# Local attention layers: where the turn of the probabilities, its copy and the copy of the values stand in the slot

## Chip, cores and metric

The kernel runs on one core of one Trainium2 chip. The metric is the device time of one execution in microseconds. Names used: TensorE (PE; its weight loads are PEld), VectorE (DVE), ScalarE (ACT), GpSimd (POOL), SyncE (SP, which only issues DMAs here).

## What is computed

A batch of 16 sequences of 128 tokens with 128 features goes through several residual blocks. The change lies in the second one, six layers of local attention with 16 heads of 64, each followed by a feed-forward block (FFN):

```python
for i in range(DEPTH):                                   # DEPTH = 6
    x = attn_layer(shift_tokens(x), Wqkv[i], q_scale[i], k_scale[i], Wo[i]) + x
    x = ffn_layer(shift_tokens(x), ln_g[i], ln_b[i], W1[i], b1[i], W2[i], b2[i]) + x

def attn_layer(x, Wqkv, qs, ksc, Wo):
    q, k, v = split_heads(x @ Wqkv)
    q = l2norm(q) * qs ; k = l2norm(k) * ksc
    q, k = rotary(q, scale), rotary(k, 1 / scale)
    sim = (q @ k.T) * 8                  # each window of 32 sees itself and the one before
    out = softmax(mask(sim)) @ v
    return out @ Wo
```

Ahead of it stand a conditioned causal attention and a rotation of images, behind it a gated linear attention and two mixtures of experts.

## The kernel before

The local layers are cut into `LOCAL` = 384 ticks t: 6 layers, 16 sequences, 4 groups of 4 heads. They run as a software pipeline over slots u. In slot u every engine runs its function `slot(u)`, in which each stage handles the tick t = u - L of that stage (`L_QKV` = 1 to `L_PROJ` = 9, line 75). The order within a slot is written out by hand on each engine, and each engine's queue runs strictly in that order; semaphores tie the engines together.

- TensorE (`pe_local`): `queries` (L1181, into `qk_ps`), `turn_probs` (L1170, transposes of the probabilities `pr` into `pTl_ps`), deferred projections, `turn_queries` (L1188, into `turn_ps`), one step of an FFN chunk, `values` (L1244, into `vl_ps`), `score` (L1209 the mask, L1215 the products), `attend` (L1233), `project` (L1198).
- ScalarE (`act_local`): the copy of the values (`vt`, L1536, for the tick whose values TensorE made one slot earlier, `L_MOVE` = 6), four exponentials (L1545), the copy of the turned probabilities (`pT`, L1554), the copy of the attention output (`oT`, L1561), the squares of queries and keys (L1568), in every fourth slot the shift of the next sequence (`xs`, L1507 and L1509), steps of the FFN (its shift `xf`, squares, Gelus), the copy of the turned queries and keys (`qkT`, L1586).
- VectorE (`dve_local`): FFN steps, the sum `qr` of the two rope products (L1398), the cosine product (L1409), `rec` (L1417), the normalization `qn` (L1425), the sums of squares (L1433, L1437), the maximum (L1445). Around a Gelu (`bursts`) it makes the copies of `pT`, `oT`, `qkT` and `vt` in ScalarE's place.
- GpSimd (`pool_local`): scaling of the probabilities by `rec` (L1597), the sine product (L1607), the power for the norms (L1617), the power of the FFN's variance (L1624).
- SyncE: after each values copy it spreads parts of `vt` into `vx` with four DMAs (L565), after the attention of the tick two before.

`vl_ps` and `pTl_ps` lie in one PSUM bank, `bank[4]` (L279). So `turn_probs` of a slot waits until the values of the slot before are copied (`v_moved`), and `values` waits until the turned probabilities of its slot are copied (`pT_moved`). `sl_ps` and `ol_ps`, the scores and the attention output, share banks too, so `maximum` waits for `attend`. The values rotate through three of four allocated buffers (`vt[t % 3]`), and the copy into one waits for the attention of tick t - 3 (`o_ready`) and for its spread.

An FFN chunk (four sequences) starts every 16 slots from u = 25. Its steps: shift 0, mean 1, squares 2, variance 3, spread 6, gate 7 to 9, Gelu 10, up 11 to 13, down 14 to 16.

Of the kernel before, what the change touches and what calls it, by code (L numbers as in the profile page):

```python
# [22 lines left out]
GROUPS = 4  # L23
# [51 lines left out]
L_QKV, L_ROPE, L_COS, L_SUM, L_TURN, L_SCORE, L_V, L_MOVE, L_EXP, L_PROB, L_PROJ = 1, 2, 3, 4, 5, 6, 5, 6, 7, 8, 9  # L75
# [181 lines left out]
def build(nc, d, out):  # L257
    with ExitStack() as ctx:
# [184 lines left out]
        def live(t):  # L443
            return 0 <= t < LOCAL

        @block.sync
        def _(sp):
# [109 lines left out]
            for t in range(LOCAL + 32):  # L557
                if live(t):
                    near, far = vt[t % 3], vx[t % 2]
# [604 lines left out]
        def pe_local(pe):  # L1164
# [56 lines left out]
            def attend(t, u):  # L1221
# [5 lines left out]
                for k, (_, lo, hi) in enumerate(SPANS):  # L1227
                    for r in range(2):
                        for pair in range(2):
                            row = slice(pair * HD, (pair + 1) * HD)  # L1230
                            at = SLOT_V[k][pair] * P + r * HD
                            values = vt[t % 3] if k == 2 * pair else vx[t % 2]
# [63 lines left out]
            def slot(u):  # L1296
                if live(u - L_QKV):
                    queries(u - L_QKV)
                if live(u - L_PROB):
                    turn_probs(u - L_PROB, u)  # L1300
# [24 lines left out]
        def dve_local(dve):  # L1325
# [129 lines left out]
            def slot(u):  # L1455
# [35 lines left out]
                if live(t) and bursts(u):  # L1491
                    dve.wait_ge(a.v_ready, TICKS + t + 1)
                    dve.wait_ge(a.o_ready, TICKS + t - 2)
                    dve.wait_ge(a.v_spread[(t - 3) % 2], 64 * ((t - 3) // 2 + 1))
                    dve.tensor_copy(vt[t % 3][:, :], vl_ps).then_inc(a.v_moved, 1)
# [8 lines left out]
        def act_local(act):  # L1504
# [23 lines left out]

            def slot(u):
                t = u - L_MOVE  # L1530
                if live(t) and not bursts(u - 1):
                    act.wait_ge(a.v_ready, TICKS + t + 1)
                    act.wait_ge(a.o_ready, TICKS + t - 2)
                    if t >= 3:
                        act.wait_ge(a.v_spread[(t - 3) % 2], 64 * ((t - 3) // 2 + 1))
                    act.copy(vt[t % 3][:, :], vl_ps).then_inc(a.v_moved, 1)  # L1536
                t = u - L_EXP
                if live(t):
# [5 lines left out]
                    for h in range(GH):  # L1544
                        ex = act.activation(pr[t % 2][:, h * BAND:(h + 1) * BAND],  # L1545
# [4 lines left out]
                t = u - L_PROB  # L1550
                if live(t) and not bursts(u) and not bursts(u - 1):
                    act.wait_ge(a.pT_ready, TICKS + t + 1)
                    act.wait_ge(a.o_ready, TICKS + t - 1)
                    act.copy(pT[t % 2][:, 0:GB], pTl_ps).then_inc(a.pT_moved, 1)  # L1554
# [28 lines left out]
                if live(t) and not bursts(u):  # L1583
                    act.wait_ge(a.qkT_ready, t + 1)
                    act.wait_ge(a.sc_ready, TICKS + t - 1)
                    act.copy(qkT[t % 2][:, :], turn_ps[:, :]).then_inc(a.qkT_moved, 1)  # L1586
            for u in range(TAIL):
                slot(u)
# [850 lines left out]
```

## Time and profile before

| | us |
|---|---|
| median of 3 runs | 2542.26 |
| lowest, highest | 2539.84, 2543.18 |
| profiled execution, its own time | 2539.52 |
| span of its trace | 2537.7 |
| granted TensorE clock, mean | 0.989 |

| stretch, us | what runs |
|---|---|
| 0 to 507 | causal attention, images |
| 507 to 560 | the pipeline of the local layers fills |
| 560 to 2180 | local layers, one slot in 3.4 to 5.6 us |
| 2180 to 2537 | linear attention and experts |

The page's lines in the section on rows are read so: an engine's busy time and its share of the span; the chain is followed back from the last instruction, at each step to what released it. "issue" in it is time for which the profile shows no releaser. In timelines a matmul's length includes its latency, so starts, not lengths, show how densely they follow each other; the chain shows the time that each adds.

### The profile page before, as it was taken

Reading aid. Unit: us, or ns where it says so; the run is one execution under the profiler, and the core shown is the slowest. Engines: PE = TensorE matmul, PEld = TensorE weight load, DVE = VectorE, ACT = ScalarE, POOL = GpSimd, SP = SyncE. Lnnn points to the kernel's source line nnn. Section 1 sums busy time; section 2 is a strip of 40 time slices with the busy share of each in tenths; the row PEclk is TensorE's granted clock in tenths of the full one; section 3 lists DMA queues with packets and bytes.
Section 4 is the critical chain, followed back from the end, with each engine's and each line's share of the span. In section 5 each row is a group of like instructions: output and inputs, shape, how many; then the busy total and the mean of one; then the engine's idle time right before and its main releaser. Section 6 shows DMA issues by size and latency. Waiting matters only on the chain.

```text
span 2537.7 us, 98074 instructions
## 1 busy us (share of the span) xinstructions
PE 2406.5 (95%) x36438; PEld 1705.4 (67%) x36442; DVE 1999.7 (79%) x4388; ACT 1885.7 (74%) x6630; POOL 1764.7 (70%) x1605
## 2 busy tenths in 40 slices
PE   7999888879999999999999999999999999799999
PEld 6888555546666666666666666666666766377874
DVE  5555699978888888888888888888888888555644
ACT  4777899868888888888888888888888888533323
POOL 2888887488888888888888878888888888122200
PEclk9999999999999999999999999999999999899999
DMA  4100210021112111211112111211121111100000
GB/s 123 15 15 15 51 14 13 10 85 37 32 34 66 38 36 33 58 42 43 33 41 59 41 33 33 66 39 36 34 58 43 42 33 34 30 1 1 1 1 17
DMA packets 177876, 91.06 MB, mean 36 GB/s; under 512 B 40974, under 2 KB 174328, under 8 KB 177408
## 3 DMA queue, kind: packets, MB, share of 16 engines
q1 hardware_dynamic: 168574, 80.42, 11.8%
q0 software_dynamic: 8192, 4.21, 1.4%
q8 instruction: 298, 4.88, 0.8%
q14 instruction: 170, 1.39, 0.2%
q10 hardware_dynamic: 642, 0.15, 0.0%
HBM read 30.57 MB, written 3.76 MB: 14 GB/s over the span
## 4 chain that ended last, share of the span: by engine, by line
PE 82%; DVE 10%; issue 5%; POOL 2%; ACT 1%; SPq 0%; DMA 0%; DVEq 0%; POOLq 0%; ACTq 0%
PE bank L1181 13%; PE bank L1198 9%; PE scores L1233 7%; PE bank L1244 7%; PE bank L1188 6%; PE scores L1215 6%; PE bank L1170 3%; PE bank L1273 3%; PE bank L1291 2%; PE bank L1282 2%; PE bank L639 2%; PE scores L1209 2%; DVE rg_prod L1011 2%; PE scores L671 2%; PE bank L1915 1%
## 5 line engine op out<-in xcount | busy, mean ns | idle before, releaser
L1617 POOL TENSOR_TENSOR rs<-ssc,neg_half 128x8 f32<-128x8 f32 x384 | 644.0, 1677 | 39.0 <-DVE ssc L1437 39.0
L1607 POOL TENSOR_TENSOR t_pair<-qn_pair,tabs 128x512 f32<-128x512 f32 x384 | 489.1, 1274 | 12.2 <-DVE qn_pair L1425 11.6
L1545 ACT ACTIVATE pr<-scores,negmax 128x64 f32<-128x64 f32 x1536 | 461.6, 313 | 48.2 <-DVE negmax L1445 23.5
L1597 POOL TENSOR_TENSOR pr<-pr,rec 128x256 f32<-128x256 f32 x384 | 235.5, 613 | 282.3 <-DVE rec L1417 282.3
L1181 PE MATMUL bank<-wqk,xs 128*128 128x512 f32 x768 | 402.5, 606 | 12.5 <-DVE qn_pair L1425 11.2
L1545 ACT ACTIVATION_READ_ACCUMULATOR pr<-scores,negmax 128x1 f32 x1536 | 311.5, 203 | 0.0
L1080 POOL DMA_INDIRECT rg_win<-rg_images,share_down x256 | 255.3, 997 | 76.7 <-issue 56.4
L1433 DVE TENSOR_REDUCE ss<-sq 128x8 f32<-128x512 f32 x384 | 260.9, 679 | 34.0 <-ACT sq L1568 32.8
L1425 DVE TENSOR_TENSOR qn_pair<-bank,rs 128x512 f32<-128x512 f32 x384 | 257.1, 669 | 27.0 <-POOL rs L1617 26.8
L1536 ACT COPY vt<-bank 128x256 f32<-128x256 f32 x361 | 135.2, 374 | 186.8 <-issue 186.5
L1198 PE MATMUL bank<-oT,wo 128*128 128x128 f32 x1536 | 266.1, 296 | 0.0
L1398 DVE TENSOR_TENSOR qr_pair<-t_pair 128x512 f32<-128x512 f32 x384 | 265.6, 692 | 0.3 <-issue 0.2
L1409 DVE TENSOR_TENSOR t_pair<-qn_pair,tabc 128x512 f32<-128x512 f32 x384 | 262.9, 685 | 0.0
L1568 ACT ACTIVATE sq<-bank 128x512 f32<-128x512 f32 x384 | 241.8, 630 | 13.9 <-PE bank L1181 13.9
L1445 DVE TENSOR_REDUCE negmax<-scores 128x4 f32<-128x256 f32 x384 | 162.9, 424 | 108.8 <-PE scores L1233 100.1
L1244 PE MATMUL bank<-wv,xs 128*128 128x256 f32 x768 | 236.6, 390 | 10.2 <-ACT pT L1554 3.2
L1170 PEld LDWEIGHTS bank<-ident,pr 128*128 128x128 f32 x768 | 107.5, 141 | 201.1 <-issue 197.8
L1188 PE MATMUL bank<-ident,qr_pair 128*128 128x128 f32 x1536 | 230.9, 273 | 0.0
L1244 PEld LDWEIGHTS bank<-wv,xs 128*128 128x128 f32 x768 | 131.8, 190 | 135.7 <-issue 132.0
L1586 ACT COPY qkT<-bank 128x512 f32<-128x512 f32 x361 | 219.4, 608 | 3.1 <-PE bank L1188 0.3
L1233 PE MATMUL scores<-pT,vt 64*64 64x64 f32 (+1 forms) x3072 | 211.8, 231 | 0.6 <-ACT oT L1561 0.4
L1198 PEld LDWEIGHTS bank<-oT,wo 128*128 128x128 f32 x1536 | 200.5, 190 | 13.3 <-issue 0.5
(313 smaller groups left out, 5503.7 us busy)
## 6 DMA issues: line engine op xcount, KB each, us to landing
rg_prod<-vt SPq DMA_DIRECT2D x1536, 32.0 KB, 1.9
wqk<-in_L_ffn_Wqkv SPq DMA_DIRECT2D x20, 256.0 KB
rg_win<-rg_images,share_down POOLq DMA_INDIRECT x256
wv<-in_L_ffn_Wqkv SPq DMA_DIRECT2D x20, 128.0 KB
wo<-in_L_ffn_Wo SPq DMA_DIRECT2D x20, 128.0 KB, 2.5
w<-in_L_ffn_W SPq DMA_DIRECT2D x6, 341.0 KB
rg_images<-rg_prod SPq DMA_DIRECT2D x1, 1625.0 KB, 7.7
ZT<-in_x SPq DMA_DIRECT2D x4, 256.0 KB, 4.0
```

Source lines behind the costliest of these rows:

```text
L1181: pe.matmul(qk_ps[t % 2][:, :], xs[b % 2][:, :], wqk[:, g, :, :].rearrange("p i n -> p (i n)"), start=True, stop=True).then_inc(a.qk_ready, 1)
L1188: mm = pe.transpose(turn_ps[:, c * P:(c + 1) * P], qr[t % 2][:, c * P:(c + 1) * P], ident[:, :])
L1198: mm = pe.matmul(yl_ps, wo[:, 2 * g + c, :], oT[b % 2][:, (2 * g + c) * P:(2 * g + c + 1) * P], start=(g == 0 and c == 0), stop=(g == GROU ...
L1233: mm = pe.matmul(ol_ps[r * HD:(r + 1) * HD, pair, lo:hi], values[row, at:at + HD], pT[t % 2][row, r * P + lo:r * P + hi], start=True, stop ...
L1244: pe.matmul(vl_ps, xs[b % 2][:, :], wv[:, g * GV:(g + 1) * GV], start=True, stop=True)\
L1398: dve.tensor_tensor(qr[t % 2][:, :], t1[t % 2][:, :], t2[t % 2][:, :], ALU.add)\
L1409: dve.tensor_tensor(t1[t % 2][:, :].rearrange("p (i h e) -> p i h e", i=2, h=GH), qn[t % 2][:, :].rearrange("p (i h e) -> p i h e", i=2, h ...
L1425: dve.tensor_tensor(heads(qn[t % 2][:, :]), heads(qk_ps[t % 2][:, :]), over(rs[t % 2][:, :], [P, 8, HD], 2), ALU.mult).then_inc(a.normed, 1)
L1433: dve.tensor_reduce(ss[t % 2][:, :, 0], heads(sq[t % 2][:, :]), AX.X, ALU.add).then_inc(a.summed, 1)
L1545: ex = act.activation(pr[t % 2][:, h * BAND:(h + 1) * BAND], sl_ps[:, h // 2, h % 2 * BAND:(h % 2 + 1) * BAND], ACT.Exp, bias=negmax[t % 2 ...
L1607: pool.tensor_tensor(t2[t % 2][:, :].rearrange("p (i h f e) -> p i h f e", i=2, h=GH, f=2), qn[t % 2][:, :].rearrange("p (i h f e) -> p i ...
L1617: pool.tensor_tensor(rs[t % 2][:, :], ssc[t % 2][:, :], neg_half[:, 0:8], ALU.pow)\
```

## The change

TensorE runs `turn_probs` ahead of `queries` in its slot. ScalarE copies the turned probabilities between its second and third exponential instead of after the fourth (where a slot has exponentials). The copy of the values moves from the head of ScalarE's next slot to the end of the slot in which TensorE makes them, behind the copy of `qkT`. The values rotate through four buffers, so their copy waits for the attention and the spread of tick t - 4. Slots next to a Gelu keep their copies on VectorE, where only the buffer and the waits of the values copy change.

```diff
-                    near, far = vt[t % 3], vx[t % 2]
+                    near, far = vt[t % GROUPS], vx[t % 2]
...
             def slot(u):
+                if live(u - L_PROB):
+                    turn_probs(u - L_PROB, u)
                 if live(u - L_QKV):
                     queries(u - L_QKV)
-                if live(u - L_PROB):
-                    turn_probs(u - L_PROB, u)
...
                     dve.wait_ge(a.v_ready, TICKS + t + 1)
-                    dve.wait_ge(a.o_ready, TICKS + t - 2)
-                    dve.wait_ge(a.v_spread[(t - 3) % 2], 64 * ((t - 3) // 2 + 1))
-                    dve.tensor_copy(vt[t % 3][:, :], vl_ps).then_inc(a.v_moved, 1)
+                    dve.wait_ge(a.o_ready, TICKS + t - 3)
+                    dve.wait_ge(a.v_spread[t % 2], 64 * (t // 2 - 1))
+                    dve.tensor_copy(vt[t % GROUPS][:, :], vl_ps).then_inc(a.v_moved, 1)
...
+            def pT_copy(u):
+                t = u - L_PROB
+                if live(t) and not bursts(u) and not bursts(u - 1):
+                    act.wait_ge(a.pT_ready, TICKS + t + 1)
+                    act.wait_ge(a.o_ready, TICKS + t - 1)
+                    act.copy(pT[t % 2][:, 0:GB], pTl_ps).then_inc(a.pT_moved, 1)
+
             def slot(u):
-                t = u - L_MOVE
-                if live(t) and not bursts(u - 1):
-                    act.wait_ge(a.v_ready, TICKS + t + 1)
-                    act.wait_ge(a.o_ready, TICKS + t - 2)
-                    if t >= 3:
-                        act.wait_ge(a.v_spread[(t - 3) % 2], 64 * ((t - 3) // 2 + 1))
-                    act.copy(vt[t % 3][:, :], vl_ps).then_inc(a.v_moved, 1)
                 t = u - L_EXP
...
                     for h in range(GH):
+                        if h == GH // 2:
+                            pT_copy(u)
                         ex = act.activation(pr[t % 2][:, h * BAND:(h + 1) * BAND],
...
                     ex.then_inc(a.exp_ready, 1)
-                t = u - L_PROB
-                if live(t) and not bursts(u) and not bursts(u - 1):
-                    act.wait_ge(a.pT_ready, TICKS + t + 1)
-                    act.wait_ge(a.o_ready, TICKS + t - 1)
-                    act.copy(pT[t % 2][:, 0:GB], pTl_ps).then_inc(a.pT_moved, 1)
+                else:
+                    pT_copy(u)
...
                     act.copy(qkT[t % 2][:, :], turn_ps[:, :]).then_inc(a.qkT_moved, 1)
+                t = u - L_V
+                if live(t) and not bursts(u):
+                    act.wait_ge(a.v_ready, TICKS + t + 1)
+                    act.wait_ge(a.o_ready, TICKS + t - 3)
+                    if t >= 4:
+                        act.wait_ge(a.v_spread[t % 2], 64 * (t // 2 - 1))
+                    act.copy(vt[t % GROUPS][:, :], vl_ps).then_inc(a.v_moved, 1)
```

## Rows read from the trace of the kernel before

**Rows 1.** The page: busy time by engine, then the chain that ended last, by engine.
```profile
PE 2406.5 (95%) x36438; PEld 1705.4 (67%) x36442; DVE 1999.7 (79%) x4388; ACT 1885.7 (74%) x6630; POOL 1764.7 (70%) x1605
...
PE 82%; DVE 10%; issue 5%; POOL 2%; ACT 1%; SPq 0%; DMA 0%; DVEq 0%; POOLq 0%; ACTq 0%
```

**Rows 2.** Busy time by stretch: window, length, then PE, PEld, DVE, ACT, POOL, clock.
```profile
560.00:2050.00 1490.00, 1462.52 (x25577) 1025.19 (x25576) 1290.02 (x2871) 1237.99 (x4753) 1223.57 (x1060) 1.00 0.16 42
```

**Rows 3.** Timeline of ScalarE in a short slot: start us, us, line, out<-in.
```profile
1040.63 0.39 ACT L1554 COPY pT<-bank 128x256 f32<-128x256 f32 x1
1040.88 0.42 ACT L1561 COPY oT<-scores 128x256 f32<-128x256 f32 x1
```

**Rows 4.** The chain that ended last: start us, length us, what ran on it.
```profile
1040.95 0.16 issue
1041.12 0.67 PE bank L1244 x2
...
1054.29 0.43 PE bank L1244 x2
...
1067.14 0.95 issue
...
2142.44 0.67 PE bank L1244 x2
```

**Rows 5.** Timelines of TensorE and ScalarE around slots 15, 0 and 1.
```profile
1087.18 0.38 ACT L1536 COPY vt<-bank 128x256 f32<-128x256 f32 x1
1091.53 0.38 ACT L1536 COPY vt<-bank 128x256 f32<-128x256 f32 x1
...
1087.42 1.02 PE L1181 MATMUL bank<-wqk,xs 128*128 128x512 f32 x2
1088.28 0.38 PE L1170 MATMUL bank<-ident,pr 128*128 128x128 f32 x2
...
1091.30 1.12 PE L1181 MATMUL bank<-wqk,xs 128*128 128x512 f32 x2
```

**Rows 6.** The same behind slot 3.
```profile
1035.09 0.38 ACT L1536 COPY vt<-bank 128x256 f32<-128x256 f32 x1
1035.33 1.02 PE L1181 MATMUL bank<-wqk,xs 128*128 128x512 f32 x2
```

**Rows 7.** Timeline of the one slot in which the turn came late.
```profile
606.65 0.38 ACT L1536 COPY vt<-bank 128x256 f32<-128x256 f32 x1
607.17 0.41 PE L1170 MATMUL bank<-ident,pr 128*128 128x128 f32 x2
607.42 0.60 PE L1188 MATMUL bank<-ident,qr_pair 128*128 128x128 f32 x4
```

**Rows 8.** Timelines of VectorE, GpSimd and TensorE in slots 4 to 7.
```profile
1036.94 0.17 DVE L1417 RECIPROCAL rec<-sums 128x4 f32<-128x4 f32 x1
1039.27 0.68 DVE L1398 TENSOR_TENSOR qr_pair<-t_pair 128x512 f32<-128x512 f32 x1
1043.23 0.73 DVE L1398 TENSOR_TENSOR qr_pair<-t_pair 128x512 f32<-128x512 f32 x1
1045.50 0.69 DVE L1425 TENSOR_TENSOR qn_pair<-bank,rs 128x512 f32<-128x512 f32 x1 [0.64 <-POOL rs L1617]
1048.08 0.55 DVE L1358 TENSOR_SCALAR rg_prod<-rg_prod,cols 128x512 f32<-128x512 f32 x1
...
1037.19 0.61 POOL L1597 TENSOR_TENSOR pr<-pr,rec 128x256 f32<-128x256 f32 x1 [1.14 <-DVE rec L1417]
1039.00 1.64 POOL L1617 TENSOR_TENSOR rs<-ssc,neg_half 128x8 f32<-128x8 f32 x1
1040.60 1.01 POOL L1624 TENSOR_TENSOR xr<-xv,neg_half 128x4 f32<-128x4 f32 x1
1043.37 2.09 POOL L1617 TENSOR_TENSOR rs<-ssc,neg_half 128x8 f32<-128x8 f32 x1
...
1048.77 1.09 PE L1273 MATMUL bank<-rg_prod,w 128*128 128x512 f32 x2
```

More of the change, by code:

```diff
@@ L72 @@
 TABLES_AT = (4, 6, 7, 8)
-L_QKV, L_ROPE, L_COS, L_SUM, L_TURN, L_SCORE, L_V, L_MOVE, L_EXP, L_PROB, L_PROJ = 1, 2, 3, 4, 5, 6, 5, 6, 7, 8, 9
+L_QKV, L_ROPE, L_COS, L_SUM, L_TURN, L_SCORE, L_V, L_EXP, L_PROB, L_PROJ = 1, 2, 3, 4, 5, 6, 5, 7, 8, 9
 FFN_FIRST, FFN_EVERY = TICKS // NCH + L_PROJ, TICKS // NCH
@@ L1231, in attend @@
                             at = SLOT_V[k][pair] * P + r * HD
-                            values = vt[t % 3] if k == 2 * pair else vx[t % 2]
+                            values = vt[t % GROUPS] if k == 2 * pair else vx[t % 2]
                             mm = pe.matmul(ol_ps[r * HD:(r + 1) * HD, pair, lo:hi], values[row, at:at + HD],
```

## Prediction

> **What bounds the kernel now.** I read the page's busy times and its chain first: TensorE is busy 95% of the span and carries 82% of the chain that ended last [rows 1]. The busy table by stretch places it: the local layers run from about 507 to 2180 us, and between 560 and 2050 us TensorE is busy 1462.5 of 1490 us at full clock, while ScalarE, VectorE and GpSimd have 1238, 1290 and 1224 us of work [rows 2]. So the change can win only what TensorE's chain loses to waits, and it can cost whatever new wait it puts into TensorE's queue. Then I read the chain piece by piece and the four timelines slot against slot. The FFN chunks repeat every 16 slots; I number the slots 0 to 15 from the one where a chunk starts (u = 25, 41, ...). There are 23 such periods.
>
> In a slot with no FFN work ahead of the values (slots 4 and 5, and most of those before u = 25), `values` waits for the copy of the turned probabilities, because both live in one bank. The copy starts behind all four exponentials at 1040.63 and ends at 1041.02 [rows 3]; the chain shows 0.16 us of nothing, then 0.67 us for the two values matmuls, where an unhindered pair takes 0.43 [rows 4]. The difference is a weight load that nothing covers. There are 58 pieces of 0.67 in the chain from 557 us to the last at 2142 [rows 4]. The other wait, 0.95 us in slot 11 [rows 4], is for exponentials that stand behind the Gelus and their table loads. The change doesn't touch it.
>
> **Part 1: the copy of the turned probabilities between the exponentials.** It then starts after two exponentials, some 0.6 us earlier, and the queue position that it takes is 0.25 us (1040.63 to 1040.88) [rows 3]. That removes both pieces of the stall: 0.13 to 0.16 us plus 0.24, say 0.37 us in each of 58 slots, 21 us. This is all that the change can win. Two such slots stand in every period (0.74 us), 14 before the first FFN chunk. The price: the last two exponentials end 0.25 us later, and with them `rec`, on which GpSimd waits.
>
> **Part 2: the turn at the head of TensorE's slot.** No work is added. But the turn waits for the values copy of the slot before (the shared bank), and in front of that wait stood the queries: the turn began 0.86 us after them (1087.42, 1088.28) [rows 5]. That 0.86 us was the cover for a late values copy. Now the queries, and all that follows in TensorE's queue, stand behind the wait.
>
> **Part 3: the values copy at the end of ScalarE's slot, four buffers.** Where ScalarE had idle time, the copy moves into it and is done well before the head. Where ScalarE is full it can't come earlier: ahead of it in the queue stand the same exponentials, copies, squares, the shifts (`xs` every fourth slot, themselves waiting for the values matmul, `xf` in slot 0) and the copy of qkT. In those slots the old copy followed the qkT copy with no gap, so the old trace shows where the new one ends:
> - slot 15: ends 1087.56, head of slot 0 at 1087.42, 0.14 late [rows 5]
> - slot 0: ends 1091.91, head of slot 1 at 1091.30, 0.61 late [rows 5]
> - slot 3: ends 1035.47, head at 1035.33, 0.14 late [rows 6]; slots 7 and 11 repeat this with 0.14 and 0.15.
>
> What a late copy costs at a head is shown by the one slot in which the turn did wait: the copy ended at 607.03, the turn began at 607.17, and the next matmuls began 0.25 us behind it, where 0.22 is usual [rows 7]. So the price is the lateness plus 0.17 us: 0.31, 0.31 and 0.32 us behind slots 15, 7 and 11. Behind slot 0 it is 0.61 + 0.17, less the 0.31 by which TensorE's head has already slipped, 0.47. Together 1.41 us per period. Behind slot 10 VectorE makes the copy, also late, but that falls into the 0.95 us wait of slot 11 [rows 4] and costs nothing; without that cover it would be 0.24. The DMAs of the spread wait for the attention of a later slot as before, so the SP queue gains and loses nothing. The fourth buffer drops waits that had ended by then in every full slot, so it is worth nothing there. The weight loads at the heads where a slot had no projection may be dearer or cheaper by 0.1 us each (three per period), which I take as zero and keep for the range.
>
> **Part 4: slots 3 to 7, where the gain should appear.** Here a second chain is as long as TensorE's. From `rec` of slot 4 (1036.94) GpSimd runs without a gap: scaling at 1037.19, rotation, power at 1039.00, the FFN's power at 1040.60, scaling, rotation, power of slot 5 at 1043.37, ending 1045.46; VectorE waited for it and normalizes at 1045.50, sums, takes the maximum, and ends the FFN's normalized input at 1048.63; TensorE's gate matmul starts at 1048.77, with 1.09 us instead of 1.02 [rows 8]. It was already late. If TensorE saves 0.74 us in slots 4 and 5, it gives all of it back at this matmul. The 0.31 us of the late copy behind slot 3 is absorbed as well. What counts is how far the chain itself moves, s. First, `rec` moves by 0 to 0.25 us (Part 1); I take 0.14, the middle, since VectorE's own work had hidden part of it. Second, the power of slot 4 took 1.64 us at 1039.00 with the rope sum starting behind it (1039.27), and that of slot 5 took 2.09 us at 1043.37 with the rope sum starting just ahead of it (1043.23) [rows 8]: a power caught behind that sum costs 0.45 us more. With the shorter slot 4 the sum comes about 0.15 us earlier and the power 0.14 later, so slot 4 would be caught too. It is decided by a few hundredths, so s is 0.14 or 0.59, and I take the mean, 0.37.
>
> The Trainium skill, page "SBUF — State Buffer", section "SBUF: two separate sides", has a rule that speaks against the change here: a VectorE instruction with two SBUF inputs and a GpSimd instruction share a pair of ports as an exclusive lock, held to the end by whichever starts first. The 1.64 and 2.09 us agree. By the rule slot 4 is caught whenever the sum is first, and the total below would be 46 us; without it, 36.
>
> **The sum.** (1.41 + 0.37) x 23 = 41 us. The 14 short slots before the chunks I take as zero: 5 us of stalls go, but there the order of exponentials, squares, sums and maximum and the same caught power come up as limits, so it is between -5 and +3. The profiled execution took 2539.5 us around a span of 2537.7; it would take 2580.5. The median of the runs lies 2.7 us above it, so I forecast 2583 us.
>
> **Rivals.**
> 1. *The GpSimd chain gives way* (22%). If slots 4 and 5 keep their 0.74 us, slot 3 costs its 0.31 openly: 1.41 + 0.31 - 0.74 = 0.98 us per period, 23 us, less 5 in the early slots: 18 us, 2560 us. Against it: the gapless run and the late gate matmul [rows 8].
> 2. *Faster* (10%). ScalarE has the values copy done before the head in the full slots. That needs it to end 0.17 us before the head or sooner, 0.31 us earlier than in the trace. If the earlier release of the bank pulled the values matmul, and with it the `xs` shift, forward by so much, all stalls at heads vanish and the 58 waits are won: 2542 - 21 = 2521 us. Against it: slots 7, 11 and 15 have FFN work ahead of `values`, which didn't wait for the bank there.
> 3. *Nothing* (5%). Heads cost less than 0.17 us, the gain of slots 4 and 5 stays in part, 2542 us.
> 4. *More of the caught power* (8%). TensorE's shorter slots bring the rope sum inside GpSimd's rotation too, VectorE is held up by up to 0.6 us more per period, and the early slots run at GpSimd's pace: 14 + 3 us more, 2600 us.
>
> **How the numbers follow.** My forecast has 55%, with its own range 2573 to 2595 (s of 0.14 or 0.59, the loads at the heads, the early slots). To leave out no more than 2 in 10 I reach down to rival 1 with its bounds and up towards rival 4: 2554 to 2598. A measurement of this kernel can tell about 0.2%, 5 us, from no change. Slower by more than that: forecast, rivals 1 and 4, 85%. Within it: 5%. Faster: 10%.
>
> **What the new profile would show.** Right: in the chain no piece of 0.67 at `values` in slots 4 and 5; a wait ahead of the turn behind slots 15, 0, 3, 7 and 11, with the values copy ending about 0.14 us before the turn starts; slot 0 to 1 the longest. GpSimd's run from slot 4 to 6 as gapless as before and TensorE waiting for the gate of slot 7 by some 0.8 us. The power in slot 4 at 1.64 or 2.09 us decides s. Wrong: the copy ends ahead of the head in the full slots (rival 2), or slot 7 stays at its length while 4 and 5 are shorter (rival 1).

## The result, and the profile after the change

| | before | after |
|---|---|---|
| median of the runs, us | 2541.11 (4 runs) | 2584.55 (4 runs) |
| lowest, highest | 2539.84, 2543.18 | 2583.42, 2585.65 |
| profiled execution, own time | 2539.52 | 2585.65 |
| span of its trace | 2537.7 | 2583.9 |
| granted TensorE clock, mean | 0.989 | 0.986 |

The change makes the kernel slower: the ratio of the times is 1.0169, with a 95% interval of 1.0157 to 1.0181. 2583 us was forecast.

The page of the kernel after, busy times and chain by engine, to be held against [rows 1]; below it the busy table of the same stretch as [rows 2].

```profile
PE 2423.9 (94%) x36438; PEld 1707.0 (66%) x36442; DVE 2009.7 (78%) x4388; ACT 1871.3 (72%) x6630; POOL 1782.1 (69%) x1605
...
POOL 38%; PE 31%; issue 15%; DVE 13%; DMA 1%; SPq 1%; ACT 1%; DVEq 0%; POOLq 0%; ACTq 0%
```

```profile
560.00:2050.00 1490.00, 1436.31 (x24968) 999.84 (x24945) 1264.63 (x2796) 1194.68 (x4635) 1208.63 (x1033) 1.00 0.16 41
```

Each engine runs the same number of instructions, and in 1490 us gets less of them done: TensorE 24968 matmuls where it was 25577. So most of the time went to waiting. Over the whole span VectorE is busy 10 us longer and GpSimd 17 us longer than before with the same instructions, which is time that single instructions were held up; the slots below show which. The chain has moved from TensorE (82%) to GpSimd (38%), with 15% of "issue". It must be read with care. In most slots its GpSimd pieces are followed by an "issue" piece of 0.45 to 1.3 us, which is GpSimd waiting for something the chain couldn't name; only where its pieces follow each other nearly without a gap is GpSimd the bound. That is in slots 4 to 6 alone.

The waits of the same stretch name the new ones (engine, line, releaser: total us, times, longest):

```profile
ACT pr L1547 <- DVE negmax L1445: 232.9, 243, 1.8
...
PE bank L1273 <- DVE rg_prod L1358: 14.1, 20, 0.8
...
PE bank L1170 <- ACT vt L1592: 9.4, 23, 1.4
```

TensorE waits at the head for the copy of the values, and at the gate matmul for the FFN's normalized input, neither of which stood among the waits of before. The ScalarE wait of 232.9 us costs nothing by itself: ScalarE used to stand idle ahead of the values copy, and now, with that copy gone to the slot's end, it stands idle ahead of the exponentials.

The rest is read best slot by slot. A slot's length here is the time from the start of the `attend` run (L1233) of the slot before it to the start of its own, so it holds its own head; a cell is the median over the 22 or 23 periods.

| slot | 0 | 1 | 4 | 5 | 6 | 7 | 8 | 9, 10, 11 together | 12 |
|---|---|---|---|---|---|---|---|---|---|
| before, us | 4.43 | 3.98 | 3.94 | 3.89 | 4.01 | 4.58 | 4.43 | 13.54 | 4.43 |
| after, us | 4.74 | 4.35 | 3.88 | 3.70 | 4.14 | 5.44 | 4.74 | 13.49 | 4.75 |
| difference | +0.31 | +0.37 | -0.06 | -0.19 | +0.13 | +0.86 | +0.31 | -0.05 | +0.32 |

Slots 2, 3 and 13 to 15 are unchanged. Summed over every slot, not by medians, the 366 slots behind the first chunk's start are 41.6 us longer: 27.7 us in slots 0, 1, 8 and 12, 15.0 us in slots 4 to 7, -1.1 us elsewhere. What lies ahead of `attend` of u = 9 adds 2.6 us, the slots u = 10 to 25 add 0.2, and what lies behind the local layers 1.7, which makes the 46.1 us between the two spans.

The heads of slots 0 and 1, timelines of ScalarE and TensorE, against [rows 5]:

```profile
1102.07 0.38 ACT L1592 COPY vt<-bank 128x256 f32<-128x256 f32 x1
1106.42 0.38 ACT L1592 COPY vt<-bank 128x256 f32<-128x256 f32 x1
...
1102.59 0.41 PE L1170 MATMUL bank<-ident,pr 128*128 128x128 f32 x2
1102.84 1.02 PE L1181 MATMUL bank<-wqk,xs 128*128 128x512 f32 x2
...
1106.94 0.41 PE L1170 MATMUL bank<-ident,pr 128*128 128x128 f32 x2 [0.37 <-ACT vt L1592]
```

The copies end at 1102.45 and 1106.80, and the turns start 0.14 us behind each. The queries stand behind the turn. Where they once ran during the last part of the copy, TensorE now does nothing.

Slots 4 to 7 of the same period, timelines of GpSimd, VectorE and TensorE, against [rows 8]:

```profile
1121.90 0.61 POOL L1603 TENSOR_TENSOR pr<-pr,rec 128x256 f32<-128x256 f32 x1 [1.02 <-DVE rec L1417]
1123.74 2.18 POOL L1623 TENSOR_TENSOR rs<-ssc,neg_half 128x8 f32<-128x8 f32 x1
1125.89 1.00 POOL L1630 TENSOR_TENSOR xr<-xv,neg_half 128x4 f32<-128x4 f32 x1
1127.44 1.27 POOL L1613 TENSOR_TENSOR t_pair<-qn_pair,tabs 128x512 f32<-128x512 f32 x1
1128.68 2.08 POOL L1623 TENSOR_TENSOR rs<-ssc,neg_half 128x8 f32<-128x8 f32 x1
...
1123.74 0.68 DVE L1398 TENSOR_TENSOR qr_pair<-t_pair 128x512 f32<-128x512 f32 x1
1127.82 1.44 DVE L1398 TENSOR_TENSOR qr_pair<-t_pair 128x512 f32<-128x512 f32 x1
1130.79 0.69 DVE L1425 TENSOR_TENSOR qn_pair<-bank,rs 128x512 f32<-128x512 f32 x1 [0.83 <-POOL rs L1623]
1133.37 0.55 DVE L1358 TENSOR_SCALAR rg_prod<-rg_prod,cols 128x512 f32<-128x512 f32 x1
...
1121.70 0.60 PE L1244 MATMUL bank<-wv,xs 128*128 128x256 f32 x2
1134.06 1.10 PE L1273 MATMUL bank<-rg_prod,w 128*128 128x512 f32 x2 [0.79 <-DVE rg_prod L1358]
```

The values matmuls of slot 4 run in 0.60 us with no stall, where the timeline of before has 0.67 us in slots 4 and 5, so the change does what it says. The power of slot 4 now takes 2.18 us where it took 1.64. From there everything is late: the power of slot 5, VectorE's normalization, the sums, the FFN's input, and TensorE waits 0.79 us for it at the gate matmul of slot 7. VectorE's rope sum of slot 5 (1127.82, 1.44 us where 0.68 is usual) started inside GpSimd's rotation (1127.44 to 1128.71) and ended 0.55 us behind that rotation: it was held up in its turn. In the kernel before, the same sum took 0.72 to 0.87 us.

The medians over the periods show how slot 4 got there, counted from the start of `attend` in slot 3. Before, `rec` came at 2.64 us, the power at 4.70 and the rope sum at 4.96, so the power led by 0.26. After, `rec` comes at 2.79, the power at 4.90 and the sum at 4.90: 0.20 us later and 0.06 us earlier use up the lead exactly.

The kernel after holds an experiment of its own. In 3 of the 23 periods the power of slot 4 was not caught. Two of them (GpSimd, then VectorE):

```profile
697.80 1.64 POOL L1623 TENSOR_TENSOR rs<-ssc,neg_half 128x8 f32<-128x8 f32 x1
697.91 0.68 DVE L1398 TENSOR_TENSOR qr_pair<-t_pair 128x512 f32<-128x512 f32 x1
...
1408.14 1.64 POOL L1623 TENSOR_TENSOR rs<-ssc,neg_half 128x8 f32<-128x8 f32 x1
1408.23 0.68 DVE L1398 TENSOR_TENSOR qr_pair<-t_pair 128x512 f32<-128x512 f32 x1
```

Here the rope sum starts 0.11 and 0.09 us behind the power; at 1123.74 both start together. Slots 4 to 7 of these three periods are together 0.15, 0.20 and 0.20 us longer than before, those of the other twenty 0.62 to 0.81 us. So one instruction pair that starts 0.1 us earlier or later decides over some 0.55 us of a period.

### The profile page after: what moved, and what is told of

Same layout as the page of the kernel before. It is cut to its first block, busy times and chain, and to the rows that moved or that the text cites. A ratio compares the mean times of both kernels' runs of the same rounds, so it can differ in the third digit from the quotient of the medians.

```text
span 2583.9 us, 98074 instructions
## 1 busy us (share of the span) xinstructions
PE 2423.9 (94%) x36438; PEld 1707.0 (66%) x36442; DVE 2009.7 (78%) x4388; ACT 1871.3 (72%) x6630; POOL 1782.1 (69%) x1605
## 4 chain that ended last, share of the span: by engine, by line
POOL 38%; PE 31%; issue 15%; DVE 13%; DMA 1%; SPq 1%; ACT 1%; DVEq 0%; POOLq 0%; ACTq 0%
POOL rs L1623 19%; POOL t_pair L1613 13%; POOL pr L1603 5%; PE bank L1273 3%; PE bank L639 2%; PE bank L1181 2%; DVE rg_prod L1011 2%; PE scores L671 1%; PE scores L1233 1%; PE bank L1921 1%; PE bank L1945 1%; DVE t_pair L989 1%; DVE qr_pair L989 1%; PE bank L686 1%; PE bank L1244 1%
## 5 line engine op out<-in xcount | busy, mean ns | idle before, releaser
L1623 POOL TENSOR_TENSOR rs<-ssc,neg_half 128x8 f32<-128x8 f32 x384 | 659.2, 1717 | 38.0 <-DVE ssc L1437 38.0
L1547 ACT ACTIVATE pr<-scores,negmax 128x64 f32<-128x64 f32 x1536 | 474.3, 320 | 275.3 <-DVE negmax L1445 271.4
L1181 PE MATMUL bank<-wqk,xs 128*128 128x512 f32 x768 | 396.7, 599 | 11.5 <-DVE qn_pair L1425 10.4
L1547 ACT ACTIVATION_READ_ACCUMULATOR pr<-scores,negmax 128x1 f32 x1536 | 318.5, 207 | 0.0
L1188 PEld LDWEIGHTS bank<-ident,qr_pair 128*128 128x128 f32 x1536 | 192.0, 141 | 189.7 <-issue 189.0
L1398 DVE TENSOR_TENSOR qr_pair<-t_pair 128x512 f32<-128x512 f32 x384 | 279.5, 728 | 0.3 <-issue 0.2
L1233 PE MATMUL scores<-pT,vt 64*64 64x64 f32 (+1 forms) x3072 | 211.8, 231 | 0.5 <-ACT oT L1560 0.3
L1233 PE MATMUL scores<-pT,rg_prod 64*64 64x32 f32 (+1 forms) x6144 | 206.7, 218 | 0.0
```

What stands on the lines that cost most here:

```text
L1181: pe.matmul(qk_ps[t % 2][:, :], xs[b % 2][:, :], wqk[:, g, :, :].rearrange("p i n -> p (i n)"), start=True, stop=True).then_inc(a.qk_ready, 1)
L1188: mm = pe.transpose(turn_ps[:, c * P:(c + 1) * P], qr[t % 2][:, c * P:(c + 1) * P], ident[:, :])
L1233: mm = pe.matmul(ol_ps[r * HD:(r + 1) * HD, pair, lo:hi], values[row, at:at + HD], pT[t % 2][row, r * P + lo:r * P + hi], start=True, stop ...
L1398: dve.tensor_tensor(qr[t % 2][:, :], t1[t % 2][:, :], t2[t % 2][:, :], ALU.add)\
L1547: ex = act.activation(pr[t % 2][:, h * BAND:(h + 1) * BAND], sl_ps[:, h // 2, h % 2 * BAND:(h % 2 + 1) * BAND], ACT.Exp, bias=negmax[t % 2 ...
L1623: pool.tensor_tensor(rs[t % 2][:, :], ssc[t % 2][:, :], neg_half[:, 0:8], ALU.pow)\
```

## The experiments

The theory had two parts. *Heads*: with the turn first, a values copy that ends behind ScalarE's full slots makes TensorE wait openly, since the queries no longer cover it. *Caught power*: the earlier release of the bank shortens slots 4 and 5, and then the power of slot 4 falls behind the rope sum on VectorE and the chain over GpSimd gives back more than was won. The rivals: the order on ScalarE itself, or the copy between the exponentials, costs the time; or the chain in slots 4 to 7 is late for another reason (the power of the FFN's variance, VectorE's own load).

**The turn first, its copy back behind the four exponentials**

```diff
                     for h in range(GH):
-                        if h == GH // 2:
-                            pT_copy(u)
...
-                else:
-                    pT_copy(u)
+                pT_copy(u)
```

> The changed kernel with the copy of the turned probabilities back behind all four exponentials; the turn stays at the head of TensorE's slot, the values copy at the end of ScalarE's. Theory (heads wait for a late values copy in the full slots): the stalls at the heads stay, 1.29 us per period as the changed kernel shows them (0.31 behind slots 15, 7 and 11, 0.37 behind slot 0), and the 0.31 behind slot 3 is now open apart from some 0.15 that slot 7 had to wait anyway. 1.45 x 23 = 33 us above before: 2574 us, 2568 to 2582; the 58 stalls at the values matmul are back. Rival (the loss comes from rec, which the copy between the exponentials makes later, and GpSimd's chain behind it): that cause is gone, so the time is that of before, 2541 us, 2537 to 2546.

Measured 2566.76 us, ratio 1.0102 (1.0085 to 1.0119). The four slots with a late copy keep their price (4.74, 4.34, 4.74, 4.75 us), and slots 4 to 7 are those of before (3.94, 3.88, 4.01, 4.59), the power of slot 4 at 1.63 us. The local layers are 27.1 us longer. So the heads alone cost 27 us, and the copy between the exponentials brings the rest of the loss. The time lies just below the expected range, 7 us below its middle. Half of that comes from counting the late copy behind slot 3 as open in every period (0.15 x 23 = 3.5 us): with the old order on ScalarE, `values` of slot 4 waits for the copy of the turned probabilities anyway, and slots 4 to 7 show nothing of the later head. Another part is the periods in which a head pays nothing.

**The turn back behind the queries as well; only the values copy stays moved**

```diff
             def slot(u):
+                if live(u - L_QKV):
+                    queries(u - L_QKV)
                 if live(u - L_PROB):
                     turn_probs(u - L_PROB, u)
-                if live(u - L_QKV):
-                    queries(u - L_QKV)
```

(The copy of the turned probabilities is as in the experiment above.)

> The changed kernel with the turn back behind the queries and its copy back behind the exponentials: only the values copy at the end of ScalarE's slot and the four buffers are left of the change. Theory (heads): the queries cover the late values copy again, so 2541 us, within 4 of before, and the difference to the run with the turn at the head is the price of the heads, some 33 us. Rival (the early values copy itself or the fourth buffer costs time on ScalarE or in the DMA queue): the loss of that run stays, above 2560 us.

Measured 2540.70 us, ratio 0.9997 (0.9988 to 1.0007), and the median of every slot is that of before. The new place of the values copy and its four buffers cost nothing. The difference to the experiment above, 26 us, is the place of the turn alone.

**All of the change, with the values copy ahead in the full slots**

```diff
+                early = u % GROUPS == 0
+                if early:
+                    v_copy(u)
                 if live(u) and u % GROUPS == 0:
...
+                if step == F_SHIFT and not early:
+                    v_copy(u)
+                    early = True
...
-                t = u - L_V
-                if live(t) and not bursts(u):
...
+                if not early:
+                    v_copy(u)
```

`v_copy` is the changed kernel's own block at the slot's end, made a function. It comes ahead of the shift `xs` in every fourth slot, and ahead of the copy of `qkT` in slot 0.

> The changed kernel with one more move: in every fourth slot ScalarE copies the values ahead of the shift of xs (which waits for the values matmul anyway), and in slot 0 ahead of the copy of qkT. Theory (heads): the copy now ends 0.3 us or more before the head everywhere, the stalls of 0.31, 0.37, 0.31 and 0.31 us go, 1.3 x 23 = 30 us: 2555 us, 2549 to 2561. The stall of slot 7 stays, since GpSimd's chain from slot 4 decides there. Rival (GpSimd's chain is the whole loss, and the stalls at the heads are only time that it would take anyway): 2580 us or more.

Measured 2557.29 us, ratio 1.006 (1.0043 to 1.0077): 27 us of the 43 are back. The copies of this kernel's slots 15 and 0, and the turns behind them:

```profile
1094.95 0.37 ACT L1536 COPY vt<-bank 128x256 f32<-128x256 f32 x1 [0.58 <-PE bank L1244]
1099.93 0.37 ACT L1536 COPY vt<-bank 128x256 f32<-128x256 f32 x1
...
1096.37 0.38 PE L1170 MATMUL bank<-ident,pr 128*128 128x128 f32 x2
1100.45 0.41 PE L1170 MATMUL bank<-ident,pr 128*128 128x128 f32 x2
```

Behind slot 15 the copy now ends 1.05 us ahead of the turn; slots 0, 8 and 12 are back at 4.43 us. Behind slot 0 it ends at 1100.30, 0.15 us ahead of a turn that still waits for it: slot 1 is at 4.11, and 0.13 us remain. Slots 4 to 7 keep their loss (3.69, 3.75, 4.14, 5.44 us, the power of slot 4 at 2.10), and they are now nearly all that is left: 13.6 of the 15.8 us by which the local layers are longer than before. The two parts of the loss are separate and add up.

**The change without the power of the FFN's variance on GpSimd**

```diff
-                    pool.tensor_tensor(xr[:, :], xv[:, :], neg_half[:, 0:CH], ALU.pow).then_inc(s.lf_rstd, 1)
```

(With the waits around it; VectorE writes `xr` in place of `xv`.)

> The changed kernel without the FFN's power on GpSimd (the inverse root of the variance is left out; VectorE writes the variance plus epsilon in its place): 1.0 us less in GpSimd's gapless run from slot 4 to slot 6, once per period. Theory (that run decides when the gate matmul of slot 7 starts): slots 4 to 7 go from 0.74 us above before towards TensorE's own length, 0.3 to 0.5 us below before, so 1.0 to 1.2 us per period, 25 us: 2560 us, 2554 to 2566, with the heads still stalling. Rival (slot 7 waits for something else, for instance for the heads before it): 2584 us, within 4.

Measured 2567.07 us, ratio 1.0107 (1.009 to 1.0124). It gets back 17 us where 24 were expected. Its slots 4 to 6 on GpSimd and VectorE:

```profile
1117.17 2.17 POOL L1623 TENSOR_TENSOR rs<-ssc,neg_half 128x8 f32<-128x8 f32 x1
1120.15 1.27 POOL L1613 TENSOR_TENSOR t_pair<-qn_pair,tabs 128x512 f32<-128x512 f32 x1 [0.23 <-DVE qn_pair L1425]
...
1119.37 0.69 DVE L1425 TENSOR_TENSOR qn_pair<-bank,rs 128x512 f32<-128x512 f32 x1 [0.32 <-POOL rs L1623]
```

The FFN's power took 1.0 us from GpSimd's run, but taking it away shortens the chain by only 0.70 us: the rotation of slot 5 can't start before VectorE's normalization, which itself waited for the caught power (2.17 us, still there). The late power is therefore on the chain by another way than GpSimd's queue. Slots 4 to 7 together take 16.45 us where the kernel before takes 16.42 with that instruction in place, so GpSimd's load alone does not explain the loss.

**The copy of the turned probabilities back behind the exponentials in slot 4 only**

```diff
+            def late_copy(u):
+                return ffn_step(u)[1] in (4,)
...
-                        if h == GH // 2:
+                        if h == GH // 2 and not late_copy(u):
...
-                else:
+                if not live(u - L_EXP) or late_copy(u):
```

(On top of the values copy ahead in the full slots.) This and all that follow ran on two other chips, on which the kernel before takes 2599 us: the stretch ahead of the local layers is some 58 us longer there (in the traces below, since the kernel before and the changed kernel were not traced on those chips), and the slots of the local layers that a kernel leaves alone have the same lengths. They are compared by ratios and by slots.

> The kernel with the values copy ahead in full slots, and in slot 4 of each period the copy of the turned probabilities back behind the four exponentials. Theory (the run on GpSimd from slot 4 decides slot 7: it starts at rec of slot 4, and its first power is caught behind the rope sum of slot 5 because slot 4 is short): rec of slot 4 is 0.11 to 0.25 us earlier, slot 4 has its old length, its power takes 1.64 again and not 2.1. Slots 4 to 7 lose nothing more against before (they are 0.60 us per period above it): 2557 - 13 = 2544 us, 2540 to 2548. Rival (slot 7 waits because slots 4 and 5 are shorter, wherever rec of slot 4 lies, or because of slot 5 alone): 2552 us or more.

Measured 2602.31 us against 2599.19, ratio 1.0012 (1.0003 to 1.0022), as expected. Slot 4 is at 3.89 us and its power at 1.64, slot 7 at 4.83 instead of 5.44. Giving 0.2 us of the gain back in one slot saves 0.6 in another. This run moves `rec` of slot 4 back as well (2.64 us behind `attend` of slot 3, as before), so it doesn't tell the later `rec` from the caught power. The idle sums below do.

**The change with an idle sum on VectorE ahead of the rope sum of slot 5**

```diff
+                if live(u) and ffn_step(u)[1] == 5:
+                    dve.tensor_reduce(idle_sum[:, 0:4], sq[u % 2][:, 0:256].rearrange("p (h e) -> p h e", e=HD),
+                                      AX.X, ALU.add)
                 turned(u - L_SUM)
```

The sum is read by nobody. It delays the rope sum by one instruction and changes nothing else.

> The changed kernel with work added: in slot 5 of each period VectorE first reduces 256 columns of old squares into a scratch tile that nobody reads, about 0.35 us, so that the rope sum starts behind the power of slot 4 and not just ahead of it. Theory (a power is held up for 0.45 us when the rope sum has started first): the power of slot 4 takes 1.64 us instead of 2.17, GpSimd's run ends 0.45 to 0.5 us earlier, slot 7 is as much shorter, and the kernel is faster though it does more: 2584.5 - 10 = 2574 us, 2570 to 2578. Rival (the longer power has another cause, such as the length of GpSimd's run without a gap): same time or up to 8 us slower, 2584 to 2592.

Measured 2633.12 us, ratio 1.0129 (1.0114 to 1.0145), against 1.0169 without the idle sum. The local layers are 33.4 us longer than before instead of 41.6: work that is added takes 8 us off them, and slots 4 to 7 alone go from 15.0 us above before to 4.9. The power of slot 4 is back at 1.64 us and slot 7 at 5.04, while `rec` comes as late as in the changed kernel (2.79). The pair in question, with the idle sum ahead:

```profile
1249.02 1.64 POOL L1627 TENSOR_TENSOR rs<-ssc,neg_half 128x8 f32<-128x8 f32 x1
...
1249.02 0.41 DVE L1479 TENSOR_REDUCE idle_sum<-sq 128x4 f32<-128x256 f32 x1
1249.35 0.68 DVE L1399 TENSOR_TENSOR qr_pair<-t_pair 128x512 f32<-128x512 f32 x1
```

The power starts at the same instant as the idle sum and takes 1.64 us. So what catches it is not VectorE at work: the sum over one input leaves it alone, the sum of two does not. This is the run that shows the cause, and the rival of VectorE's load falls with it.

All 14 traces agree, power by power. From the start of the local pipeline on, they hold 617 powers over 8 columns that started while VectorE's rope sum or cosine product (both operands in SBUF) was running or started level: 616 of them took 2.08 to 2.18 us. The other one took 1.63, with the sum 0.01 us behind. None of the other powers took over 1.70, and among these are some 600 that started while VectorE ran an instruction with one operand in PSUM (L1354, L1375 and L1389 of the kernel before): 1.63 to 1.65 us. The price goes by what the VectorE instruction has still to run: with 0.59 us left it is 0.45, with 0.68 left 0.54, and with 0.20 left (the scaling of the cosine table, 70 times) 0.05, so it is the rest less 0.14 us.

**The same, on top of the values copy ahead, with a second idle sum in slot 6**

The edit adds `tensor_reduce` over 512 columns where `ffn_step(u)[1] == 6`, to free the power of slot 5 too.

> The kernel with the values copy ahead in full slots, with idle sums on VectorE: 256 columns ahead of the rope sum of slot 5, 512 columns ahead of that of slot 6 (0.35 and 0.69 us). Theory: neither the power of slot 4 nor that of slot 5 is caught, 0.9 us per period off GpSimd's run, so that slot 7 keeps 0.3 us per period of what slots 4 and 5 save: 2557 - 20 = 2537 us, 2532 to 2543, some 4 us faster than before. Rival (the added sums delay VectorE's own way to the gate as much as they free GpSimd): 2550 us or more.

Measured 2607.26 us, ratio 1.0033 (1.0022 to 1.0045): not what was expected. The power of slot 5 and the rope sum that should have been behind it:

```profile
1244.16 2.09 POOL L1640 TENSOR_TENSOR rs<-ssc,neg_half 128x8 f32<-128x8 f32 x1
...
1243.45 0.68 DVE L1482 TENSOR_REDUCE idle_sum<-sq 128x8 f32<-128x512 f32 x1
1244.04 0.72 DVE L1399 TENSOR_TENSOR qr_pair<-t_pair 128x512 f32<-128x512 f32 x1
```

The idle sum was too short: the rope sum still leads by 0.12 us, and that is enough for the whole price. Slot 7 gets down to 5.13 us only. Slots 4 to 7 together are at 16.57 us: with the power of slot 4 free and the copy still between the exponentials, 0.15 us above before remains, about what the later `rec` was taken for (0.14).

**The same, with the idle sum in the early slots too**

The condition becomes `ffn_step(u)[1] == 5 or 8 < u < FFN_FIRST`.

> As the one before, with the 256-column idle sum also in slots 9 to 24, before the first FFN chunk, where slots take 4.08 us against 3.93 before. Theory (there too the power is caught behind the rope sum in every slot): these 16 slots go to 3.7 to 3.8 us, 4 to 6 us less: 2533 us, 2527 to 2539. Rival (those slots are bound by the order exponentials, squares, sums, maximum, which the idle sum lengthens): no faster, or up to 5 us slower than the one before.

Measured 2602.42 us, ratio 1.001 (1.0001 to 1.0019), 5 us less than the run above. The median of the slots before the first chunk falls from 4.11 us in the run above (4.08 in the changed kernel, 3.93 before) to 3.75. There, too, powers were caught: 13 in the changed kernel and 19 in the run above, against 4 before, and 6 here.

**Longer in slot 6: 512 and 256 columns**

```diff
+                if live(u) and ffn_step(u)[1] == 6:
+                    for w in (512, 256):
```

> As the run with idle sums in the early slots and slots 5 and 6, but in slot 6 the idle sum is 768 columns instead of 512. In the 512-column run the rope sum of slot 6 still started 0.12 us ahead of the power of slot 5, which took 2.09 us. Theory (who starts first decides): now it starts about 0.25 us behind the power, which takes 1.64; 0.45 us per period less: from 1.001 of before to 0.997, 10 us less. Rival (the 2.09 us of slot 5 come from GpSimd's run without a gap): the power stays at 2.09, the ratio at 1.001 or up to 1.004.

Measured 2588.37 us against 2598.89, ratio 0.9961 (0.9948 to 0.9974): as expected, faster than the kernel before, and the fastest of all the kernels here. Powers and rope sums of slots 4 and 5:

```profile
1162.86 1.63 POOL L1642 TENSOR_TENSOR rs<-ssc,neg_half 128x8 f32<-128x8 f32 x1
1167.24 1.63 POOL L1642 TENSOR_TENSOR rs<-ssc,neg_half 128x8 f32<-128x8 f32 x1
...
1163.10 0.68 DVE L1399 TENSOR_TENSOR qr_pair<-t_pair 128x512 f32<-128x512 f32 x1
1167.44 0.68 DVE L1399 TENSOR_TENSOR qr_pair<-t_pair 128x512 f32<-128x512 f32 x1
```

Both sums start behind their power, by 0.24 and 0.20 us, and both powers take 1.63 us. Slot 7 is at 4.67 us (before 4.58, after 5.44), and slots 4 and 5 keep their gain at 3.70 and 3.75. The local layers are 5.3 us shorter than before behind u = 25, and u = 10 to 25 another 3.2 us.

**A useful step in place of the idle sums**

VectorE makes the FFN's normalized input (L1354, L1358) in slot 6 ahead of `qn`, not at the start of slot 7, on top of the values copy ahead.

```diff
-                if c is not None:
+                if c is not None and step != F_SPREAD:
                     ffn(c, step)
...
                     inverse(u - L_EXP)
+                    c, step = ffn_step(u)
+                    if step == F_SPREAD:
+                        ffn(c, step)
                     normed(u - L_ROPE)
```

> The kernel with the values copy ahead in full slots, and VectorE makes the FFN's normalized input (the product with the spread root and the scale and shift, 0.68 and 0.55 us) in slot 6 ahead of qn, where it waits for GpSimd anyway, instead of at the start of slot 7. Theory (the loss in slots 4 to 7 is only the late gate matmul at the end of GpSimd's run): slot 7 falls from 5.44 us to 4.5 to 4.7, the saving of slots 4 and 5 shows at last, 18 us less than the run with the values copy ahead alone: 0.999 of before, 0.997 to 1.001. Rival (TensorE would wait in slot 7 for the scores or queries instead, which hang on the same run): slot 7 above 5.0 us, ratio above 1.003.

Measured 2608.87 us, ratio 1.0038 (1.0025 to 1.0051): a miss. The gate matmul hardly waits any more, as expected (1.9 us in all where it was 15.6 in the changed kernel), but slot 7 is still at 4.99 us:

```profile
1181.54 2.08 POOL L1636 TENSOR_TENSOR rs<-ssc,neg_half 128x8 f32<-128x8 f32 x1
...
1181.07 0.42 DVE L1445 TENSOR_REDUCE negmax<-scores 128x4 f32<-128x256 f32 x1
1181.41 0.72 DVE L1398 TENSOR_TENSOR qr_pair<-t_pair 128x512 f32<-128x512 f32 x1
...
1181.53 0.31 ACT L1559 ACTIVATE pr<-scores,negmax 128x64 f32<-128x64 f32 x1 [1.98 <-DVE negmax L1445]
...
1183.50 0.27 PE L1209 MATMUL scores<-local_mask,ident 128*128 128x128 bf16 x2 [0.24 <-ACT oT L1572]
```

The maximum now stands behind the FFN's step, the exponentials wait 1.98 us for it, the copy of the attention output stands behind them, and the scores of slot 7 wait for that copy. The power of slot 6 is caught as well, by a sum 0.13 us ahead of it. The wait had only moved from one of VectorE's outputs to the next.

**That step with idle sums in slot 5 and the early slots**

> The one before, with the idle sum of 256 columns on VectorE in slot 5 and in slots 9 to 24. Theory: the power of slot 4 isn't caught, slot 6 and 7 lose their last 0.1 to 0.3 us, and the early slots go from 4.08 to 3.75 us: 4 + 4 us less than the one before, ratio 0.996, 0.993 to 0.998. Rival: no faster than the one before.

Measured 2607.11 us, ratio 1.0033 (1.002 to 1.0046), a miss for the same reason: the power of slot 4 is at 1.63 us, that of slot 6 at 2.08, slot 7 at 5.17.

**That step in the kernel before**

> The kernel before, with the same move of the FFN's normalized input into slot 6 alone. Theory (in the kernel before the gate matmul of slot 7 is late by 0.15 us): slot 7 goes from 4.58 to 4.43 us, 3.4 us in all, ratio 0.9987, 0.997 to 1.0. Rival (the gate matmul isn't late there, or the move costs VectorE elsewhere): 1.0 or more.

Measured 2615.59 us, ratio 1.0062 (1.0049 to 1.0074), where a small gain was expected. Slot 7 goes from 4.58 to 5.09 us, the power of slot 6 from 1.64 to 2.08, and VectorE waits 21 times, 0.55 us each, for the broadcast matmul (L1263) of the same slot. So the place of that step is bad by itself, with or without the change.

## Why the prediction was right

The median was forecast to within 2 us, and where the loss arises was right. The sum was not as good as that. Against it the heads cost 4.7 us less and slots 4 to 7 6.5 us more; the fill, u = 10 to 25, the other slots and what lies behind brought 3.4 us that it didn't have. That makes the profiled execution 5 us longer than forecast (2585.65, 2580.5). And the median lies 1.1 us below that execution, where the old one lay 2.7 us above its own. That these errors cancel to less than 2 us is luck; that the loss is some 40 us, in the heads and at the gate of slot 7, is not.

- **Heads.** Three terms of 0.31, 0.31 and 0.32 us: measured 0.31, 0.31 and 0.32 us in slots 0, 8 and 12. Moving only the turn back gave back 26 us, and moving only the values copy ahead 27; these two experiments show the cause. Behind slot 0 the step said 0.47, and from the head of slot 0 to that of slot 1 there are indeed 0.47 us more (4.35 against 3.88 between 1087.42 and 1091.30 [rows 5]). But the slot grew by 0.37: the queries at that head had taken 1.12 us instead of 1.02 in the old trace, in a row that was quoted, and that 0.10 us went away. The step read the start of that row and not its length. Also, not every period pays: behind slot 7 six of the 23 pay 0.1 us or nothing, and three behind slot 11. The sum is 27.7 us where 1.41 x 23 = 32.4 were forecast.
- **The 0.74 us of slots 4 and 5 given back** at the gate matmul of slot 7, with TensorE waiting some 0.8 us there: right, 0.79 us.
- **Behind slot 3** the late copy's 0.31 us was said to be absorbed. About half of it is. The kernel with the values copy ahead doesn't pay it, and its slots 4 to 7 take 17.02 us together, the changed kernel's 17.16, those of before 16.42. So 0.14 us of it is not absorbed.
- **The chain's shift s.** 0.14 or 0.59 us were given as the two cases and 0.37 as their mean. No period was at the mean: three stand at 0.15 to 0.20 and twenty at 0.62 to 0.81, 15.0 us in all where 8.5 were forecast. The mis-sized term is the mean. The prediction's own numbers had the sum start 0.27 us behind the power (1039.27, 1039.00 [rows 8]), then come 0.15 us earlier and the power 0.14 us later, which puts the sum 0.02 us ahead; by its own rule that is a caught power, 0.59 us. Without the late copy behind slot 3 the chain does move by 0.60 us (17.02 less 16.42); the 0.14 us of slot 3 comes on top and gives the usual 0.74. The margin was as thin as the prediction said: the pair starts level, and with the sum 0.09 us later the power was free.
- **The rule of the Trainium skill**, page "SBUF — State Buffer", section "SBUF: two separate sides": a VectorE instruction with two SBUF inputs and a GpSimd instruction that reads SBUF take a shared pair of ports as an exclusive lock, which whichever starts first holds to its end. The traces agree where VectorE comes first: 2.08 to 2.18 us with the two-input sum ahead or level, 1.63 to 1.65 with it behind or with a one-input sum in its place. They agree for GpSimd's rotation, too, whose end the sum inside it waited for. They do not agree for the power: by the rule a power that starts first would hold VectorE to its end, but in the 14 traces VectorE's sum or cosine product started some 7400 times inside a power of 1.64 us and took 0.67 to 0.73 us each time. The pairs at 697.80 and 1408.14 show it (0.68 us). The measurement decides: a power that is ahead costs VectorE nothing, which is why letting it go first pays. Of the two totals that the prediction set against each other, 46 us by the rule and 36 without it, the slots bear out the first in the term that hangs on it: 0.65 us per period on average, near to 0.59 and not to 0.14.
- **Early slots** were taken at zero between -5 and +3. u = 10 to 25 cost 0.2 us together. The stall went and the caught power came: with idle sums there they are 3.1 to 3.2 us shorter than before.
- **Rival 1**, the GpSimd chain gives way, would have left slot 7 at its length; it grew by 0.86 us. **Rival 2** needed the copy to come 0.31 us earlier in the full slots; it comes at the same place. Its mechanism is real, though: once the copy is put ahead there, the heads cost 0.13 us per period. **Rival 4** was right on its mechanism, VectorE held inside the rotation, but not on its size.
- **Rival 3** needed heads below 0.17 us; they cost 0.31 and more.
- **The fill**, a term at nothing. `attend` of u = 9 comes 2.6 us later (541.8 to 544.5 us). 1.4 us of it is the slot u = 9 itself, 5.52 us where it was 4.14: its turn waits 0.72 us for the values copy, and between 540 and 543 us TensorE's granted clock was 0.58 where it was 1.00 before. With the turn at the head and its copy back it is 5.41 us, with the turn back as well 4.14, and with the values copy ahead 4.41. So this is one more late head, which the prediction left out. The other 1.3 us stands ahead of `attend` of u = 8; the first matmul of the local layers (L1181) already starts 1.8 us later (509.5, 507.8), and from 507.1 to 511.2 us in the first four experiments, so it is not put down to the change.
- **Open:** 1.7 us behind the local layers. From the last `attend` to the end the changed kernel takes 357.1 us and the kernel before 355.4. The first four experiments, which keep this part of the program but for the last FFN's power in one, take 354.5 to 355.2, so no run ties the 1.7 us to the change. In the first 80 us of that stretch the granted clock was 0.81 after, 0.85 before and 0.85 with the turn's copy back.

## What to carry to other kernels

A wait can be moved ahead of independent work only where what it waits for is early; list the slots in which the releasing engine is full, and read how late each one is, before moving. When a fixed-order pipeline has a second chain just behind the first, shortening the first changes which instruction of a pair starts first on the engines that share ports, and that can cost more than was won; the start times of the pairs, to 0.1 us, decide it. Where two cases are that far apart, take the one that the starts point to, not their mean.

## What the runs showed of the hardware

- A GpSimd power over 8 columns takes 1.63 to 1.65 us alone and 2.08 to 2.18 us when VectorE's sum of two SBUF operands started ahead of it, even by 0.12 us, or level with it. With the sum 0.09 us behind it is free (and in one case with 0.01 us). VectorE's one-input sum (256 columns, same start) left it at 1.64 us, and so did VectorE instructions with one operand in PSUM (some 600 times).
- The price is what VectorE's instruction has still to run when the power starts, less 0.14 us: 0.45 us for 0.59, 0.54 for 0.68, 0.05 for 0.20.
- The other way it depends on GpSimd's instruction. VectorE's sum, 0.68 us alone, took 1.44 us when it started inside GpSimd's rotation (128x512), and ended 0.55 us behind it. Inside a power over 8 columns it took 0.67 to 0.73 us every time.
- Idle work can therefore make a kernel faster: idle sums (three in each period, one in each slot from u = 9 to 24) turned a ratio of 1.006 into 0.9961, each against the kernel before on its own chip.
- The same program took some 57 us longer on other chips (2599 against 2542 us). In the kernel before with the FFN's step moved, the first attention of the local layers came at 596 us, where it is 538 in the kernel before on the first chip; its untouched local slots have the old lengths.
